# A pixel-transformer block sequence on one core: the order of six streams' steps written anew

## The reference, cut to what matters

```
x: (128, 64, 128), cond: (128, 128), ctx: (128, 64, 128)
L0: x += gate * attend(q, k, v of LN(x) * (1 + scale) + shift) @ W   (gate, scale, shift: silu(cond) @ W + b)
    x += attend(q of LN(x), k and v of ctx) @ W
    x += gate * gelu((LN(x) * (1 + scale) + shift) @ W1) @ W2
L1: x += attend(q of modulated LN(x), k and v of modulated LN(ctx)) @ W
L2: as L0, with k and v of its cross attention from LN(ctx)
L3: n = LN(x) * gamma + beta;  e = softmax(n Wq (ctx Wk)^T / sqrt(128)) (ctx Wv)
    c = [n, e, cond];  routed = sum over 3 experts of softmax(c Wr) * (silu(c W1) @ W2 + b2)
    out = x + sigmoid(silu(c G1) @ G2) * (routed @ Wo + bo)
attend: softmax(q k^T / sqrt(8)) v, per head
```

## Time and profile before

| | |
|---|---|
| median of 3 runs | 1714.29 us (1711.70 to 1717.39) |
| profiled execution: its time, its span | 1715.89 us, 1714.1 us |
| granted TensorE clock, mean | 0.996 |
| PE, DVE, ACT, POOL busy | 1620.7, 1516.9, 1413.6, 766.4 us |
| instructions on PE, DVE, ACT, POOL | 31141, 4240, 3650, 1335 |
| transfers | 41.23 MB, 24 GB/s in the mean |

### The profile page before, as it was taken

The page is one execution under the profiler, slowest core; times in us unless marked ns, Lnnn a source line. Parts: engine busy times, 40 slices in busy tenths (PEclk is TensorE's granted clock), DMA queues, the critical chain, the costliest instruction groups (busy, mean ns, idle before and its releaser), DMA issues.

```text
span 1714.1 us, 74561 instructions
## 1 busy us (share of the span) xinstructions
PE 1620.7 (95%) x31141; PEld 1395.1 (81%) x31141; DVE 1516.9 (88%) x4240; ACT 1413.6 (82%) x3650; POOL 766.4 (45%) x1335
## 2 busy tenths in 40 slices
PE   6988999999999999999999999999999999999998
PEld 5876788888778888888888888888888888887887
DVE  6988898998899989899999999998899898899865
ACT  3766888888788978888898988888798888787886
POOL 4434444444453444444454444444444444454441
PEclk9999999999999999999999999999999999999999
DMA  7000000000000000000000001000100000000000
GB/s 237 3 22 2 19 24 24 24 15 12 24 25 24 18 9 25 24 24 24 14 14 24 25 25 24 24 7 21 31 18 24 25 15 18 18 15 15 3 2 20
DMA packets 57787, 41.23 MB, mean 24 GB/s; under 512 B 13552, under 2 KB 56176, under 8 KB 57328
## 3 DMA queue, kind: packets, MB, share of 16 engines
q1 hardware_dynamic: 57456, 36.46, 7.4%
HBM read 31.99 MB, written 4.46 MB: 21 GB/s over the span
## 4 chain that ended last, share of the span: by engine, by line
PE 55%; DVE 26%; ACT 9%; issue 5%; POOL 3%; DMA 1%; SPq 1%; DVEq 0%; POOLq 0%
PE half L967 7%; PE half L1091 6%; DVE top L1267 6%; PE half L1010 6%; PE half L995 5%; DVE n_rows L1231 5%; PE half L1026 4%; PE half L1036 4%; PE half L1100 4%; PE half L844 3%; PE half L1019 3%; PE half L943 3%; ACT pT L1456 3%; PE half L947 3%; PE half L954 3%
## 5 line engine op out<-in xcount | busy, mean ns | idle before, releaser
L1267 DVE TENSOR_REDUCE top<-half 128x32 f32<-128x2048 f32 x160 | 365.3, 2284 | 28.9 <-PE half L967 26.3
L1456 ACT ACTIVATE pT<-half 128x512 f32<-128x512 f32 x640 | 328.5, 609 | 60.3 <-PE half L995 58.4
L786 POOL TENSOR_TENSOR rstd<-shifted,minus_halves 128x2 f32<-128x2 f32 x256 | 183.0, 717 | 318.0 <-DVE shifted L1226 315.8
L1231 DVE SCALAR_TENSOR_TENSOR n_rows<-x_rows,moments,rstd 128x128 f32<-128x128 f32 x512 | 205.9, 444 | 22.1 <-POOL rstd L786 20.5
L1491 ACT ACTIVATE pT<-half,mod 128x64 f32<-128x64 f32 x896 | 195.0, 341 | 27.3 <-PE half L1091 26.0
L1429 ACT ACTIVATE k_heads<-half,key_bias,own_head_sb 128x256 f32<-128x256 f32 x320 | 163.2, 573 | 41.5 <-PE half L947 39.9
L812 POOL TENSOR_TENSOR top<-top 128x32 f32<-128x32 f32 x160 | 40.5, 253 | 347.1 <-DVE top L1267 347.1
L967 PE MATMUL half<-k_heads,q_heads 32*128 32x128 f32 x5120 | 185.7, 281 | 3.8 <-ACT v_cols L1440 1.9
L1440 ACT ACTIVATE v_cols<-half 64x128 f32<-64x128 f32 x640 | 175.3, 274 | 15.7 <-PE half L954 9.5
L803 POOL TENSOR_TENSOR o_rows<-q_heads,inv_sum 128x256 f32<-128x256 f32 x160 | 101.9, 637 | 187.7 <-DVE inv_sum L1277 186.9
L995 PE MATMUL half<-q_heads,k_heads 32*128 32x128 f32 x5120 | 181.8, 276 | 2.5 <-issue 2.5
(11 more groups left out here) (150 smaller groups left out, 3707.3 us busy)
## 6 DMA issues: line engine op xcount, KB each, us to landing
gates<-gate_store SPq DMA_DIRECT2D x128, 128.0 KB, 3.1
x_rows<-x SPq DMA_DIRECT2D x32, 128.0 KB, 2.9
c_rows<-context SPq DMA_DIRECT2D x32, 128.0 KB, 2.4
out<-n_rows SPq DMA_DIRECT2D x32, 128.0 KB, 1.9
w_sb<-weights SPq DMA_DIRECT2D x1, 1856.0 KB, 7.5
w_sb<-weights SPq DMA_DIRECT2D x2, 512.0 KB, 6.6
logit_bias<-logit_store SPq DMA_DIRECT2D x64, 1.5 KB, 3.5
row_sb<-rows SPq DMA_DIRECT2D x1, 769.5 KB, 8.2
```

The lines of the kernel that those rows point to most:

```text
L786: nc.gpsimd.tensor_tensor(rstd[s][:, :], shifted[s][:, :], minus_halves[:, 0, :], ALU.pow).then_inc(rstd_in[s], 1)
L1231: m = nc.vector.scalar_tensor_tensor(out=n_rows[s][:, t, :], in0=x_rows[s][:, t, :], scalar=moments[s][:, t, 0:1], in1=rstd[s][:, t:t + 1] ...
L1267: nc.vector.tensor_reduce(term[s][0], halves[HALF_OF[n]][:, :, :].rearrange("p g (c k) -> p g c k", k=SEQ), AX.X, ALU.max).then_inc(tops_r ...
L1456: nc.scalar.activation(turn_cols[s][:, g, :], halves[HALF_OF[n]][:, g, :], ACT.Exp, scale=ATT_SCALE).then_inc(scores_read, 1)
```

## The change

Only the string `SEQUENCE` is another: it has the same digits in another order (4626 steps, each stream's own steps in the same order). The instructions, their sizes, tiles and `HALVES` are the same. The order was searched anew under one more condition: DVE's steps with two operands in SBUF are kept from running beside POOL's bulk steps.

```diff
 SEQUENCE = (
-    "24f13f0522021f1120220110100120f0022001f10021123322003f321002001ff32202020031030f132f3200231032221410"
+    "42f01f20020f211002f1002001121210503202110222f311312003f3230002301f0f2f0220100002310322f322244f010123"
...
 )
```

More of the change, by code:

```diff
@@ L257 @@
-    "4150014401211405113111410040010144010150011151131000013100531101151501451001110130101513031012101000"
-    "10040103420001150134000010"
+    "42f01f20020f211002f1002001121210503202110222f311312003f3230002301f0f2f0220100002310322f322244f010123"
+    "32211042f123314104104123110004404f1f3f01000f0233200f15433000f100430043021010233522400112011343230111"
+    "4210321015123011320110211113121004311040154000301212010031004032130222321404420241313311001100021122"
+    "0010000031010221010120150403241040030213000200101031121240122101312122200013401011023301203210020001"
@@ new lines @@
+    "3202304310003012303001435120033415155211111435222112255312221423242344512444341525232431113041043235"
+    "3321035544102453030021105553113535123155540420134425300121414511141253320333424145001204052402213403"
+    "3333204552500343352230555542205223514504434502510452444054352253424022140504410025554210522003415120"
+    "4153253350112221250111225021311332304344512454041040345453510451435253054405205213053513305253054301"
+    "1150143043153502311114310133150325025541532004303301553233350120325255203234144004124055444542210531"
@@ new lines @@
+    "4314012445101115412440402011033134050004012232501021410021241023424212124142404214520155443443404524"
+    "5341020353500045453430313312554130300522210054233100025252304255531245244205333320523553135350521133"
+    "2225235021345252135144151515523501012301411051434325104050044203421300424330021151442013531410324031"
+    "0011305201323512245325142324024112410402442400413304342104230234331030005505152033501412055011543133"
+    "2111143055212152225531222124344224351352223434235414114133201343542103454150231132511350415533050253"
@@ new lines @@
+    "0155542440213544244315024411024510330213330200111514052042210343032453502335043335203555542025235125"
+    "2444000352410544442130242020340524205524554015451542102053413255024311251202212553011121235330244011"
+    "2434523414544003410301554513540034550552541023535013535230450213115034201324512331353121034110312310"
+    "5450520515430033015335330013535220300441455242104242425545401441132053441511101541204004241105330114"
+    "0003403251220023311401021241204242524142241042143152404543353314024445340055052004414513030302550134"
@@ new lines @@
+    "5312005232310020554302222355152542052433302325415203544113354335015342521214253351521503225150405530"
+    "2541124314115340412035040220131040324330210331134325101100410021430531350212442125454321253241125344"
+    "2043142020104304021043202030331435001005230545311134512050314512311051455113225122325521242244243235"
+    "2422414421145313514123403555213445301335523145123530033555011530132104243240144050203141145110122145"
+    "3202440103521402432530343330030324535250433352232052545055231425451440003024455154420045342525354555"
@@ new lines @@
+    "2142425010214104202002213145230545253310122125011225102311144434303514243450403011434055513453000455"
+    "5503135403135352325545100131510340233111241151300003032054313155352425235142300153233321404555405314"
+    "0253202042140325524441504314132120514530111532140030321014504103304041340235220021410431021240124242"
+    "1524142241053421411244503053425444440502055300441450312355340100352202105030023055413222255531254022"
+    "5334302235151201533153550325315112135335150403512250210553514122324241245401344032512500454043313400"
@@ new lines @@
+    "2344032101413413205310410002311043315125012524523541422341201235442431202041030440421402020353533135"
+    "4505512330400001432010415321530111141322211252553121442432242235224244412154111335432034125534034213"
+    "5350323305301530305151215413155541230044024541301142145110112425330434012250314025403223040032333455"
+    "3520433352035250554252231205050014443215254042042400402342502534451045405154554205230245151122214522"
+    "5232350132215021441330434253144131114503311050504535300415505541424543150351303534523251300115040312"
@@ new lines @@
+    "2415331351341132110010345512500535240323031302353351202023350525234154004142404545242540143411205314"
+    "4511101541202400414150433031103003402152303203214103021212404142124412422041452334041524554140245545"
+    "4243415310520330514533010204025023002305002055531025322152542203532330523551555212312233235031505522"
+    "5241233441514015130455531145044125324101513434220005014440213040334211103014140230313413201001134055"
+    "3350224432125355442214214214243344204231532232433132413250504020054053025225154523120525533200422120"
@@ new lines @@
+    "2110130002154040224143512104140451410003420355040145523135530535405512013545300513101302050134401335"
+    "1403301104515412044134231444525125044512145301300011141005001521015225241101001111150453203531521351"
+    "3014142515410104153541145434535423110555021045043521040305041120131351140211101515231241001555130250"
+    "3015005515035421213512315001155014211230315130510210341440411523114241114444501411525451012554315235"
+    "2545550145553004213051204332013400301011540101111202115400354153401412515024254414534013534545040534"
@@ L259 @@
+    "5001115500003101454044051104001450455315523135143235434051344455115550351454534404353150445531344554"
+    "1340143041101135113011023310001103300110011111051002515003104110115140141501011010011150101443231305"
+    "01150410000000011015000100"
 )
```

## The result

The changed kernel takes 1693.60 us (median of 4 runs, 1692.69 to 1699.14), the kernel before 1714.79 us in the same comparison. The ratio is 0.9881, with a 95% interval of 0.9862 to 0.9900: 21 us faster (17 to 24 by the interval), where 8 were forecast. 1693.6 us lies just inside the prediction's range of 1692 to 1721, but in the part that went to rival 3 and got 0.12. The profiled execution took 1699.14 us and is the slowest of the four, so its trace shows 16.7 us of the 21.

A forecast was written before the change was run, and what follows sets the result against it. TensorE, busy 1620.7 of 1714.1 us, bounds the kernel, and VectorE now and then fails to feed it. 0.40 x 23 = 9 us saved, 1 given back: 1714.3 - 8, predicted 1706 us; range 1692 to 1721.

The forecast's parts named there:

- rival 3: VectorE the true feeder: all 58 us count, 40% comes back, 23 us, 1691; chance 0.12, with all between it and forecast.
- The place and the cause: At L1231, VectorE's normalisation passes are held up by GpSimd's bulk steps reading SBUF; 49.7 us blocked there.
- The two pairs named from the order: Normalisation pairs: `n_rows3` falls from 1.62 to 0.61 us; beside `lifted0`, 0.52 us is lost again.
- "Third, the share that the new order removes": Share of blocking at VectorE's normalisations removed by the new order: 40%, low end 17%; 0.40 x 23 = 9 us.
- The stricter of my two counts: Bulk instruction straight behind the step's own `rstd` with little VectorE work between: 47 before, 39 now, 17% fewer.
- the looser one: Steps of `normal` with a GpSimd bulk step within four steps ahead: 67 before, 40 now, 40% fewer.
- "Second, what of it is on the path ... I take 23 us": Blocked VectorE time that lengthens the run: 21 to 58 us, taken as 23, nearest TensorE's 22.6 us wait for `n_rows`.
- the prediction's sum: All that blocking costs VectorE: L1231 49.7, L1297 4.9 and L1374 3.5 us, in all 58.1 us.
- "I give back 1 us to the next waits": With `n_rows` earlier, TensorE's waits on `nT` (6.3 us) and `top` (5.6 us) take back 1 of 9 us.
- "Everything else costs nothing": Table loads (209 before, 208 now), PSUM alternation, SP's transfers, stores and last expert steps cost nothing by the orders.
- The rule that I set against the trace: Any GpSimd SBUF read, so also `rstd`, blocks L1231; avoiding bulk steps reaches two thirds, 5 us not 8. Not followed.
- The test that I named: If time falls by far more than L1231's busy time, the search found something other than contention; account wrong in kind.

The follow-up runs named there:

- hold-ups: 81 VectorE fills at normalisations, GpSimd's bulk steps made write-only: kernel before 1716.70 us (same places), 1716.91 (others); the change's order, same normalisations, 1711.34.
- the kernels with fills: GpSimd's bulk steps replaced by fills of about their length that only write (output wrong): kernel before 1675.29 us, changed kernel 1672.64 us.
- the runs with equal hold-ups: Kernel before, GpSimd's bulk steps write-only, the same 81 VectorE fills at the normalisations held up before or at 81 others: 1716.70 and 1716.91 us.
- GpSimd's waits: GpSimd's colliding bulk steps wait until the normalisation has run: kernel before, 84 places, 1693.58 us; changed kernel, 87 places, 1679.63 us.
- the combined version: Changed kernel with the first 506 steps of the order before, normalisation with two scalars per row, and GpSimd waiting at colliding bulk steps: 1674.41 us.

## Why the prediction was wrong, step by step

- The place and the cause: right. The two pairs named from the order came out at 0.57 us and with 0.47 us lost, and without GpSimd's reads no pass is long.
- "Third, the share that the new order removes", 40%: nearly right. L1231 was to fall by 20 us and fell by 19.1; of the 58.1 us it is a third, since L1297 did not profit as I had assumed. The stricter of my two counts, 17%, was far off. No run tests the looser one, which fitted, so its fit may be luck.
- "Second, what of it is on the path ... I take 23 us": this is the step that failed. By taking the blocking away it is 39 us of 58 (0.67), or of L1231's own 53.1 (0.74). Put back it is 0.79 of the time put in, and TensorE's wait for `n_rows`, from which I took the 23, is 27.3 us in a kernel that pays 41. With 0.74 to 0.79 in place of 0.4, the 19 us less of L1231 make 14 to 15 us, and with the 3 to 5 us of the order itself one is at 17 to 20, where 21 was measured (17 to 24 by the interval). The rest may be spread, or the 5.5 us of L1226 and L1207, which the prediction's sum left out; this stays open.
- "I give back 1 us to the next waits": small either way; `nT` grew by 1.3 us.
- "Everything else costs nothing": off by the 3 to 5 us by which the order seems to be better in itself (clear of the spread only with hold-ups, and barely). The prediction took this from counts of single things, which can't show it.
- The rule that I set against the trace: the row was right. In the trace before, 69 instructions of L1231 run beside nothing on GpSimd but an `rstd`; they take 342 ns in the mean and 367 at most, against 342 and 353 for the 193 with GpSimd idle. In the kernels with fills `rstd` still runs, and no pass is long; and the share that keeping bulk steps away reaches is not two thirds. Taking away the bulk steps' reads alone brings L1231 to 152.8 us, below its 156.2 us alone.
- Rival 3 (VectorE the true feeder, all 58 us) was the nearest in mechanism; I gave it 0.12 because TensorE's two largest waits for VectorE were only 28.9 us. That was the same error again: all its waits for VectorE were 45.0 us, and what its busy time hides may come on top.
- The test that I named ("if the time falls by far more than L1231's busy time, my account is wrong in kind") came close to striking, 21 against 19, and the runs with equal hold-ups and with no blocking show that the account was right in kind.

The rate is not one number. For each us less of L1231 the run became shorter by 0.64 us with GpSimd's waits in the kernel before, by 0.74 with all blocking gone from it, and by 0.63 with all blocking gone from the change (21.0 us for 33.5); for each us put in it became longer by 0.79. The spread of the medians allows for up to about 0.1 in each. Whether the rate falls as TensorE bounds more and more (it is busy for 1608.3 of 1673.9 us in the combined version) is not shown.

## What to carry to other kernels

When an engine that feeds the bound one is itself near 90% busy, count the time that it loses at 0.6 to 0.8, as measured here, not at what the bound engine is seen to wait for the one result: part of the cost shows in its waits for other results (10 of 28 us here), and part shows in no wait (its busy time fell by 12 us). Look for contention as one line's instructions of equal size with a long tail (345 ns in the middle, 1137 at most) and test it by making the suspect only write. When you put the time back by hand, count how much later the held instructions start and not the busy time of the fillers. If two engines collide, a semaphore wait on the one with room (GpSimd, 45% busy), at just the colliding places, can do what a new order of everything does.

## What the runs showed of the hardware that I had not expected

- A VectorE instruction with a single tensor from SBUF and two scalars per row (128x128, float32) takes 342 ns in the middle, much like the one with two tensors (345 and 346), and is held up by GpSimd's bulk steps as well, to 892 ns. The Trainium skill, page "SBUF — State Buffer", section "Who interferes with whom", names this operation among those that can contend, in a mode with two ports. The collision agrees with it. A gain in speed does not show here.
- Fills by GpSimd, which read nothing, held up no pass: 341 ns in the mean, 379 at most. The same section of the Trainium skill's page "SBUF — State Buffer" says that a VectorE instruction with two SBUF inputs contends with GpSimd instructions that read SBUF and not with those that only write it. The trace agrees.
- GpSimd's `rstd` (128x2, 0.71 us) reads SBUF, and the 69 instructions of L1231 beside it alone took 342 ns in the mean, as with GpSimd idle. Here that section of the Trainium skill and the trace differ, and the trace decides; why is not shown.
